# A two-layer attention and expert kernel: the first norm in portions, a bias moved, first rows loaded sooner, zeros multiplied at other places

## The reference, cut to what matters

```
x  = L0_attn_x
xn = layernorm(x)
x  = x + attention0(xn) + ffn0(xn)      # 16 heads of 8, causal; 8 experts, top 2, capacity 40
xn = layernorm(x)
x  = x + attention1(xn) + ffn1(xn)      # 16 heads, 4 key/value heads, rotary; 8 experts, top 2, no capacity
```

## Time and profile before

| | us |
|---|---|
| median of 3 runs (lowest to highest) | 489.29 (489.16 to 491.45) |
| the profiled execution | 488.85 |
| its span in the trace | 487.1 |
| PE busy | 443.3 (91%) |
| DVE busy | 317.0 (65%) |
| ACT busy | 240.2 (49%) |
| POOL busy | 188.0 (39%) |

### The profile page before, as it was taken

How to read it: one execution, slowest core, us unless ns; L and a number is a source line. 1 busy time by engine, 2 the same in 40 slices (tenths; PEclk the granted TensorE clock), 3 DMA queues, 4 the chain that set the end, 5 groups by cost and what they waited for, 6 DMA issues and landing times.

```text
span 487.1 us, 10025 instructions
## 1 busy us (share of the span) xinstructions
PE 443.3 (91%) x3323; PEld 304.5 (63%) x3325; DVE 317.0 (65%) x956; ACT 240.2 (49%) x565; POOL 188.0 (39%) x234
## 2 busy tenths in 40 slices
PE   7778899998989999999999998999988999999985
PEld 3444446665656667565665655556548999988642
DVE  4674770107668778776876789767655777765664
ACT  2421355455655655555554544445454555554662
POOL 6580121003353453553636441657611544445000
PEclk9985999999999999999999999999998999999998
DMA  5454452434464573642256443143241221211242
GB/s 175 125 120 137 125 135 61 112 86 129 139 151 128 133 177 119 140 116 65 87 161 191 153 138 93 41 130 93 68 126 54 58 75 54 80 44 34 62 130 89
DMA packets 55216, 52.76 MB, mean 108 GB/s; under 512 B 5312, under 2 KB 50000, under 8 KB 55168
## 3 DMA queue, kind: packets, MB, share of 16 engines
q1 hardware_dynamic: 44208, 35.12, 26.2%
q10 hardware_dynamic: 8528, 12.03, 8.7%
q0 software_dynamic: 2432, 5.01, 3.4%
HBM read 33.09 MB, written 19.04 MB: 107 GB/s over the span
## 4 chain that ended last, share of the span: by engine, by line
PE 65%; DVE 12%; DMA 9%; issue 5%; ACT 4%; SPq 2%; POOL 1%; ACTq 0%; DVEq 0%
PE ps_P L1652 7%; PE ps_N L1783 6%; PE ps_N L1585 5%; PE ps_P L1793 3%; PE ps_M L1793 3%; PE ps_N L1591 3%; DVE NM L1163 3%; PE ps_M L1824 3%; PE ps_S L1616 3%; PE ps_S L1783 3%; PE ps_M L1695 3%; PE ps_N L1596 3%; DMA scm<-MS 3%; PE ps_S L1630 2%; PE ps_P L1686 2%
## 5 line engine op out<-in xcount | busy, mean ns | idle before, releaser
L907 ACT ACTIVATE PT<-ps_S 128x512 f32<-128x512 f32 x192 | 112.6, 593 | 111.1 <-PE ps_S L1630 67.4
L1163 DVE TENSOR_REDUCE NM<-ps_N 128x2 f32<-128x512 f32 (+1 forms) x192 | 128.4, 682 | 50.9 <-PE ps_N L1591 32.5
L759 POOL TENSOR_SCALAR_AFFINE_SELECT PT<-PT 128x512 f32<-128x512 f32 x80 | 51.1, 663 | 128.1 <-ACT PT L907 128.1
L1585 PE MATMUL ps_N<-maskb,identb 128*128 128x256 bf16 (+1 forms) x192 | 61.0, 318 | 3.5 <-DVE NM L1163 2.2
L825 POOL DMA_INDIRECT yt<-LATE,EI x39 | 38.5, 987 | 57.0 <-DVE LATE L1403 47.7
L1652 PE MATMUL ps_P<-PT,VA 128*16 128x256 f32 (+1 forms) x1024 | 54.0, 328 | 0.4 <-ACT PT L907 0.4
L1591 PE MATMUL ps_N<-NS 96*128 96x512 f32 x96 | 51.1, 537 | 0.0
L1596 PE MATMUL ps_N<-NS 96*128 96x256 f32 (+1 forms) x128 | 49.4, 427 | 0.0
L1630 PE MATMUL ps_S<-NS 100*128 100x512 f32 (+1 forms) x96 | 46.3, 486 | 0.0
L1652 PEld LDWEIGHTS ps_P<-PT,VA 128*16 128x16 f32 x1024 | 23.3, 96 | 34.6 <-issue 20.8
L1009 ACT ACTIVATE LATE<-ps_N,ucol 128x128 f32<-128x128 f32 x104 | 29.7, 368 | 26.6 <-PE ps_N L1783 26.2
(11 more groups left out here) (196 smaller groups left out, 851.3 us busy)
## 6 DMA issues: line engine op xcount, KB each, us to landing
scr<-XQ SPq DMA_DIRECT2D x24, 256.0 KB
NS<-scr SPq DMA_DIRECT2D x64, 96.0 KB
ROT<-in_L_ffn_W SPq DMA_DIRECT2D x16, 256.0 KB, 3.1
EW<-in_moe ACTq DMA_DIRECT2D x8, 512.0 KB, 3.8
scr<-XQ SPq DMA_DIRECT2D x24, 128.0 KB
NS<-scr SPq DMA_DIRECT2D x8, 384.0 KB
TS<-scr ACTq DMA_DIRECT2D x8, 384.0 KB
TS<-scr ACTq DMA_DIRECT2D x32, 96.0 KB
```

What stands on the lines that cost most here:

```text
L759: last = pool.affine_select(out=v, in_=v, compare_op=ALU.is_ge, fill=0.0, base=0, pattern=[[0, 4], [1, P]], channel_multiplier=-1)
L907: act.activation(PT[:, n % NPT, r, :], bank[s][:], ACT.Exp, scale=SCALE).then_inc(exp_ok, 1)
L1163: dve.tensor_reduce(to, x, AX.X, ALU.max, negate=True).then_inc(nm_ok, 1)
L1585: mm(diag, identb[:], maskb[:, None, :].broadcast_to((P, many, P)), start=True, stop=False, skip_group_check=True)
```

## The change

- `first_norm`: tiles 4 to 15 are treated in two portions, 4 to 7 and 8 to 15, each with its own moments, `rsqrt` and `standardise`. Both moments still come before the copies and `low(0, 0)`.
- The bias of layer 0 is no longer added in POOL's prologue but where POOL meets the item `ffn`, after step `t=2`, and it waits for the last dispatch copy (`xd_ok`).
- A new item `rows` at `t=15, u=6`: SP waits there for the 32 scatters and loads groups 0 and 1; `moe` starts with group 2. It stands ahead of `mrow(b,0)` in SP's queue.
- `rank` uses bank M1 in place of M0.
- In `moe` on DVE, `weights(j)` comes ahead of `places(j // 4)`.
- Zeros: 12 in place of 16 at `t=1, u=0`, and 4 more at each of `t=1, u=1` and `t=1, u=2`, ahead of those units' `nat`. At the end 3 each at `(17,5)`, `(17,7)`, `(18,2)`, `(18,4)` and `(18,6)`, in bank N0.

```diff
-                plan += [("warm", "S1", 16), ("cum",), ("keys",)]
+                plan += [("warm", "S1", 12), ("cum",), ("keys",)]
...
+            if t == 1 and u in (1, 2):
+                plan.append(("warm", "S1", 4))
...
+            if t == MOE_AFTER and u == 6:
+                plan.append(("rows",))
...
+            if (t, u) in ((2 * NB + 1, 5), (2 * NB + 1, 7), (2 * NB + 2, 2), (2 * NB + 2, 4), (2 * NB + 2, 6)):
+                plan.append(("warm", "N0", 3))
...
     if kind == "rank":
-        return [("M0", item)]
+        return [("M1", item)]
...
+            def first_rows():
+
+                sp.wait_ge(scat_w, 16 * 2 * NT)
+                for g in range(2):
+                    load_group(g)
...
             def moe():
-                sp.wait_ge(scat_w, 16 * 2 * NT)
-                for g in range(NGRP):
+                for g in range(2, NGRP):
                     load_group(g)
...
-            rsqrt(slice(4, NT), rstd_ok)
+            rsqrt(slice(4, 8), rstd_ok)
+            pool.wait_ge(mv_ok, 2)
+            rsqrt(slice(8, NT), rstd_ok)
             pool.wait_ge(xn_ok, NT)
             zeros(2)
             zeros(3)
-            pool.wait_ge(wo_in, 16 * 2)
-            pool.tensor_tensor(X[:], X[:], bob[0][:, None, :].broadcast_to((P, NT, C)), ALU.add).then_inc(xbo_ok, 1)
...
+            def bias0():
+
+                pool.wait_ge(wo_in, 16 * 2)
+                pool.wait_ge(xd_ok, NB)
+                pool.tensor_tensor(X[:], X[:], bob[0][:, None, :].broadcast_to((P, NT, C)), ALU.add).then_inc(xbo_ok, 1)
+
             for item in plan:
+                if item[0] == "ffn":
+                    bias0()
...
-                moments(range(4, NT), mv_ok)
-                dve.wait_ge(mv_ok, 1)
+                moments(range(4, 8), mv_ok)
+                moments(range(8, NT), mv_ok)
+                dve.wait_ge(mv_ok, 2)
...
                 dve.wait_ge(rstd_ok, 1)
-                standardise(range(4, NT))
+                standardise(range(4, 8))
+                dve.wait_ge(rstd_ok, 2)
+                standardise(range(8, NT))
...
+                    weights(j, ats[j])
                     if j % GRP == 0:
                         places(j // GRP)
-                    weights(j, ats[j])
```

More of the change, by code:

```diff
@@ L659, in attention @@
                         zero_rows(item[1])
+                    if item[0] == "rows":
+                        first_rows()
                     if item[0] == "ans":
@@ L729, in rsqrt @@
                 pool.tensor_scalar(vpe[:, tiles], mv[:, tiles, 1], EPS, 1.0, ALU.add, ALU.mult).then_inc(pstep, 1)
-                pool.wait_ge(pstep, 2 if tiles.start == 0 else 3)
+                pool.wait_ge(pstep, {0: 2, 4: 3, 8: 4}[tiles.start])
                 pool.tensor_tensor(rstd[:, tiles], vpe[:, tiles], mhalf[:, tiles], ALU.pow).then_inc(done, 1)
@@ L1321, in slots_a @@
             def slots_a():
-                await_full(dve, "M0", ("rank",))
-                dve.tensor_copy(cumt, bank["M0"][:, 0:(NT + 1) * E1].rearrange("p (i e) -> p i e", e=E1)).then_inc(cum_ok, 1)
+                await_full(dve, "M1", ("rank",))
+                dve.tensor_copy(cumt, bank["M1"][:, 0:(NT + 1) * E1].rearrange("p (i e) -> p i e", e=E1)).then_inc(cum_ok, 1)
                 dve.wait_ge(cum_ok, 1)
@@ L1752, in rank @@
             def rank():
-                await_free(pe, "M0", ("rank",))
+                await_free(pe, "M1", ("rank",))
                 pe.wait_ge(selx_ok, 1)
-                o = M0[:, 0:(NT + 1) * E1].rearrange("p (i e) -> p i e", e=E1)
+                o = M1[:, 0:(NT + 1) * E1].rearrange("p (i e) -> p i e", e=E1)
                 mm(o[:, 0:1, :], trib[:], selb[:, 0:1, :], start=True, stop=True)
@@ L1760, in rank @@
                        skip_group_check=True)
-                mm(o[:, 1:, :], trib[:], selb[:, 1:, :], start=False, stop=True, skip_group_check=True).then_inc(full["M0"], 1)
+                mm(o[:, 1:, :], trib[:], selb[:, 1:, :], start=False, stop=True, skip_group_check=True).then_inc(full["M1"], 1)
             def moe():
```

## The result

The changed kernel took 482.75 us (median of 4 runs, 482.19 to 485.94) against 490.27 (4 runs, 489.16 to 491.45) beside it: ratio 0.9884, 95% interval 0.9841 to 0.9926. By the medians it is 7.5 us faster, by the ratio 5.7 us (3.6 to 7.8). The forecast was 477.2, with a range that ended at 482.0: the direction was right, and of the 11.9 us that were forecast some 4.4 (by the medians) did not come. The profiled execution took 482.42 (span 480.7), so it is 6.4 us shorter than the one before.

What follows compares the result with a forecast made beforehand. PE's queue was taken as the bound through most of the kernel; 0.8 + 1.9 + 3.1 + 0.3 + 3.8 + 1.6 + 0.4 = 11.9 us off 488.85 gave 476.95, predicted as 477.2, range 474.8 to 482.0.

Steps and rivals of the forecast that it cites:

- F: Expert loop on DVE: weights ahead of places spares `up` the wait in eight group-heading tiles; gain 1.6 us, bounds 0 and 2.1.
- E: Start of the experts: rows loaded sooner cut PE's pause and keep the clock up; gain 3.8 us, bounds 1.0 and 4.4.
- A: First norm in portions: POOL's power runs beside DVE's moments, so scaling starts sooner; gain 0.8 us, bounds 0 and 1.1.
- B: Bias off the prologue: DVE's cast in the router's chain no longer stalls; gain 1.92 us, bounds 1.4 and 2.1.
- G: Zeros at the end: the last projection runs at full clock; gain 0.4 us, bounds -0.3 and 0.5.
- Rival 3: Prologue: the cast was slow for another reason, so the bias move gains 0; 479.1 us, chance 4%.
- C: Step t=1: zeros in units 1 and 2 keep PE's clock at 2.4 GHz; gain 3.1 us, bounds -1.0 and 3.5.
- rival 1: Step t=1: the clock falls all the same, so the zeros there gain 0; 480.3 us, chance 15%.
- Rival 4: Half clock from step t=1 lasts until the expert loop, making the kernel slower; 490.5 us, chance 3%.
- D: `rank` in bank M1: it no longer waits for DVE's value copy out of M0; gain 0.3 us, bounds 0 and 1.2.
- rival 2: Experts' start: rows hidden anyway or late, half clock stays, gain only 1.0; 480.0 us, chance 12%.

Runs made afterwards that it cites:

- e9: The changed kernel with the places between the two copies of a tile's weights: 477.54 us, ratio 0.9766 to the kernel before.
- e7: The changed kernel with the bias of layer 0 back in POOL's prologue: 483.43 us, ratio 0.9883 to the kernel before.
- e8: The changed kernel with the first norm's later tiles in one portion again: 485.33 us, ratio 0.9931 to the kernel before.
- f1: The changed kernel run again, in turn with two other orders of places and weights: 490.12 us, the kernel before 496.55 on this occasion.
- e1: The changed kernel with the old order, places ahead of weights: 479.88 us, ratio 0.976 to the kernel before.
- f2: The changed kernel with the old order, places ahead of weights, run in turn with f1: 486.29 us, the kernel before 496.55 on this occasion.
- e12: The changed kernel with places between the weight copies and the row address loaded a tile ahead: 478.49 us, ratio 0.9817 to the kernel before.
- e2: The kernel before with only the order of weights and places swapped: 492.18 us, ratio 1.0034.
- e3: The kernel before with only the first two groups of rows loaded sooner, at step 15, unit 6: 484.36 us, ratio 0.9862.
- e4: The kernel before with only the bias of layer 0 moved ahead of the expert loop: 488.33 us, ratio 0.9939.
- e5: The changed kernel with 16 zeros ahead of `cum` and none in units 1 and 2: 483.13 us, ratio 0.9854 to the kernel before.
- e6: The kernel before with only the zeros of step t=1 split 12, 4, 4: 487.67 us, ratio 0.9966.
- e10: e9 with only group 0 of the experts' rows loaded early, group 1 with the others: 479.68 us, ratio 0.9818 to the kernel before.
- e11: The changed kernel in its own order, tile j+1's address loaded ahead of tile j's places: 480.79 us, ratio 0.9865 to the kernel before.
- f3: The changed kernel with places between the weight copies, run in turn with f1 and f2: 486.55 us, the kernel before 496.55 on this occasion.

## Why the forecast failed

Step **F** failed: "two small DVE operations stand ahead of the copy that `up` waits for", so 1.6 us would go. Two operations were counted, and what stands behind them in DVE's queue at the new place was not. In the kernel before they stood behind the address load of their own tile and cost 0.22 us of their 0.33 there; that reading, 0.2 a group, was right, and e9, which takes them away, gains 1.5 us. Moved behind the weights they hold back the address load of the next tile, from 0.25 to 0.76 us after the W2 copy's start, and the W1 copy with it. I wrote that the places "then stand before `evict`, which they did already", and asked nothing of what is queued behind `evict`. The bounds, 0 and 2.1, left out a loss. Measured in the loop: +2.36 us instead of -1.6, an error of 4.0. Some 0.6 more lie in the head: `up` of tile 1 comes 1.88 to 1.89 us after that of tile 0 with the weights first (e7, e8, f1) and 1.30 to 1.31 with the places first (e1, f2), all at full clock.

By the medians F's 4.0 is nearly the whole miss: 11.9 less 4.0 is 7.9, and they moved by 7.5. That it fits so well is partly luck. In the profiled execution 6.4 us came of 11.9; there F missed 4.0 and E 3.0, and some 1.5 came from elsewhere (A, B and G a little over the forecast, inputs that landed sooner, steps that happened to be shorter).

The other steps, from the profiled executions:

- **A**: 1.04 for 0.8. The second power was to be ready in time and was; DVE lost nothing by the split. Scaling began at 15.99 inside POOL's power (14.86 to 16.62) and took 3.15 us against 3.17. The Trainium skill (SBUF — State Buffer, Who interferes with whom) has one of the two wait where both want the shared ports; for this pair of operations no run shows it, while the cast beside the bias (e7) agrees with it. The prediction's figure for a wait, 0.5, was itself off: with a power that ends at 17.2, 0.3 would have been left of A.
- **B**: from scaling's start to the first dispatch matmul 17.82 (33.81 - 15.99) against 19.93 (37.47 - 17.54): 2.1 for 1.9. Rival 3 fell. The bias in its new place was hidden, as forecast. But this term moves with the clock too. In the ten executions with the bias moved and 12 zeros, the stretch is 17.6 to 17.8 where the half clock around the router lasted 3.4 us (seven), and 18.3 to 19.0 where it lasted 6.8 (e1, e12, f2): B was 0.9 to 2.3. "They don't bind", said of the 12 zeros, held in eight of the ten; in e12 and f2 `cum` starts 0.6 and 1.1 us after `selb` is done.
- **C**: from there to the expert loop 33.64 against 36.78: 3.1 for 3.1. The mechanism was only half right. The spell at half clock in step t=1 lasted 13.7, 13.7 and 10.2 us with neither edit near it (before, e2, e3; stretch 36.6 to 36.8), 6.8 us with the bias moved alone (e4; 35.4), 0 with the bias moved and no zeros in the units (e5) or the zeros without the bias (e6, e7), and 0 (after, e10, e12, f1, f2) or 3.4 us (e1, e8, e9, e11, f3) with both, with stretches of 33.6 to 34.8. So the changes near it shorten the spell, by 2.0 to 3.2 us of the stretch, but which of the two does it isn't settled by one execution of each, and both together don't rule it out. The Trainium skill (TensorE: Matmul & The Clock Gate, What's actually happening) says that one kernel can differ in this from run to run; the spread agrees. So rival 1 happens in part, in some executions of the changed kernel. Rival 4 was not seen.
- A, B, C and the inputs, which landed 0.5 sooner by chance, put the expert loop 6.8 us earlier. Some 0.4 of it went again by step t=5.
- **D**: `rank` runs without a wait; its step t=12 takes 20.6 us for 21.0. 0.35 for 0.3.
- **E**: head 12.40, 12.22, 13.85 and 14.37 with the load unmoved (before, e2, e4, e6), 9.87 on average over the 13 of the table: 3.3 for 3.8, or 2.5 against the kernel before alone. The load was issued as early as forecast; what was taken as fixed, its 2.85 us, is not. In the changed kernel's own profiled execution the term was 0.8: rival 2, by a late landing. It had 12%; a late landing came in 3 of 13 (after, e10, f3), and half clock at the experts' start in 3 (after, e5, e10), at 10.6 to 11.6 us of head.
- **G**: the last projection 0.68 for 1.13: about 0.5 for 0.4. No run has these zeros alone. In all twelve executions with them it takes 0.68 us, without them 1.13 to 1.20 in four (before, e2, e4, e6) and 0.68 in one (e3), so here too the clock can hold without them.

## What to carry to other kernels

Before you move an instruction off the path, ask what stands behind it at its new place: here two short operations, of which the second waits for the first, came to stand ahead of an address load that had run beside a copy. Count register loads as work of the queue that stands behind everything issued before them. Look for a place where the engine waits anyway (between the copies), and give such a term a bound on the other side of nothing.

A term that rests on the clock or on one DMA's landing, read from one profiled execution, is a draw and not a constant.

## What the runs showed of the hardware

- From the start of an address load into DVE's register to the copy that uses it 0.74 us pass when nothing stands between; 0.30 of them are the load (e1, after). It starts 0.25 us after the start of the copy ahead of it, and 0.76 with the places between. With the load done ahead, the copy starts 0.21 us after the eviction's start (e11).
- A cast on DVE that began inside POOL's bias addition ended 0.04 us after it, in five of five executions, after 0.69 to 2.27 us; with the bias moved the same cast took 0.18 to 0.26.
- The first rows' load from HBM landed after 2.75 to 3.3 or after 4.2 to 4.5 us, nothing between: 13 and 4 of 17 executions, unmoved and moved.
- The spell at half clock came in lengths of 0, 3.4, 6.8, 10.2 or 13.7 us in one and the same step.
- The expert loop repeats to 0.08 us over occasions on which the whole kernel differs by 7 us (72.02 and 72.01, 75.87 and 75.88, 73.46 and 73.54).
